# Routing inside cross-attention, four shared-expert groups ahead of the blocks, silu transposes a block later, four result pairs

## The reference

```
x = x + attn(layernorm(x))        # delta-rule attention and a gated MLP of width 512
x = x + xattn(layernorm(x), ctx, ctx, mask)   # 16 heads of 16, 375 keys per row
x = x + ffn(layernorm(x))

def ffn(x):                       # N_EXPERTS = 6, TOP_K = 2
    probs = sigmoid(xt @ gate_w.T + gate_b)
    w, idx = top_k(probs, 2);  w = w / (sum(w) + 1e-08)
    y = sum over e of ge[:, e] * ((silu(xt @ ew1[e].T) * (xt @ ew3[e].T)) @ ew2[e].T)
    z = (silu(xt @ fc1.T) * (xt @ fc2.T)) @ fc3.T      # the shared expert, for all tokens
    return y + z
```

## Time and profile before

| | |
|---|---|
| runs | median 1516.21 us of three (1514.62 to 1520.04) |
| profiled execution | 1508.45 us, its span 1506.7 us |
| busy over the span | PE 1323.7 us (88%), DVE 914.1 (61%), ACT 651.0 (43%), POOL 420.4 (28%) |
| mean granted TensorE clock | 0.931 |
| chain that ended last | PE 68%, DVE 8%, issue 7%, POOL 7% |

### The profile page before, as it was taken

How to read it: one execution, slowest core, us unless ns; L and a number is a source line. 1 busy time by engine, 2 the same in 40 slices (tenths; PEclk the granted TensorE clock), 3 DMA queues, 4 the chain that set the end, 5 groups by cost and what they waited for, 6 DMA issues and landing times.

```text
span 1506.7 us, 33730 instructions
## 1 busy us (share of the span) xinstructions
PE 1323.7 (88%) x11138; PEld 1181.8 (78%) x11138; DVE 914.1 (61%) x2823; ACT 651.0 (43%) x1474; POOL 420.4 (28%) x387
## 2 busy tenths in 40 slices
PE   5899999999898699999999999999974538898997
PEld 5888998898887588888888888888764427777886
DVE  5677567557545366666666666666656624544577
ACT  3534334434332255555555555555531214444532
POOL 2323224223312311111111111111116642332353
PEclk9999999999898699999999999999975559999999
DMA  7799100000002545455555555554114322322255
GB/s 181 156 225 231 48 0 0 0 0 0 20 11 49 144 120 117 118 119 119 119 120 118 119 119 119 119 119 118 45 32 131 109 68 75 93 79 84 80 129 168
DMA packets 117837, 143.96 MB, mean 96 GB/s; under 512 B 24112, under 2 KB 101280, under 8 KB 117744
## 3 DMA queue, kind: packets, MB, share of 16 engines
q1 hardware_dynamic: 111024, 127.21, 36.2%
q0 software_dynamic: 6160, 15.69, 3.1%
q10 hardware_dynamic: 576, 0.07, 0.0%
HBM read 75.61 MB, written 42.15 MB: 78 GB/s over the span
## 4 chain that ended last, share of the span: by engine, by line
PE 68%; DVE 8%; issue 7%; POOL 7%; SPq 3%; DMA 2%; ACT 2%; POOLq 0%; DVEq 0%; ACTq 0%
PE psum L725 19%; PE psum L961 7%; PE psum L1124 6%; PE psum L995 5%; PE psum L976 5%; PE psum L981 5%; POOL routed_h L671 4%; PE psum L1143 3%; SPq L465 2%; PE psum L846 2%; PE psum L832 2%; PE psum L933 2%; PE psum L843 2%; PE psum L1133 2%; PE psum L1022 1%
## 5 line engine op out<-in xcount | busy, mean ns | idle before, releaser
L1824 DVE CUSTOM_DVE_ANT_0 junk<-psum,biasq 112x375 f32<-112x375 f32 x512 | 270.2, 547 | 114.6 <-PE psum L961 77.5
L1432 ACT ACTIVATE pr<-psum 125x448 f32<-125x448 f32 x384 | 202.4, 544 | 115.1 <-PE psum L981 106.6
L981 PE MATMUL psum<-qst,kst 97*125 97x224 f32 x768 | 226.0, 353 | 0.0
L961 PE MATMUL psum<-kst,qst 96*112 96x376 f32 x512 | 185.9, 371 | 12.4 <-DVE smax L1824 10.8
L981 PEld LDWEIGHTS psum<-qst,kst 97*125 97x125 f32 x768 | 146.4, 191 | 7.9
L976 PE MATMUL psum<-flagk,negbig 125*125 125x448 bf16 x384 | 139.2, 363 | 3.5 <-DMA qst<-negm 3.3
L566 POOL TENSOR_TENSOR rs<-rs,neg_half 112x1 f32<-112x1 f32 x32 | 18.2, 569 | 386.8 <-DVE rs L1802 386.8
L961 PEld LDWEIGHTS psum<-kst,qst 96*112 96x112 f32 x512 | 91.3, 178 | 42.1 <-DVE smax L1824 37.2
L686 POOL DMA_INDIRECT routed_y<-yb,yrow x61 | 59.1, 969 | 146.9 <-DVE yrow L2086 117.9
L995 PE MATMUL psum<-pr,vaug 125*32 125x112 f32 x3072 | 93.7, 262 | 0.0
L995 PEld LDWEIGHTS psum<-pr,vaug 125*32 125x32 f32 x3072 | 70.3, 110 | 15.3 <-issue 6.3
(11 more groups left out here) (308 smaller groups left out, 3381.8 us busy)
## 6 DMA issues: line engine op xcount, KB each, us to landing
kst<-khi SPq DMA_DIRECT2D x64, 376.0 KB, 5.2
routed_h<-in_route_pad SPq DMA_DIRECT2D x6, 3640.0 KB, 43.2
kst<-klo SPq DMA_DIRECT2D x32, 376.0 KB, 6.8
ctxT<-in_ctxT SPq DMA_DIRECT2D x32, 375.0 KB, 5.2
hblk<-routed_h SPq DMA_DIRECT2D x61, 130.0 KB, 2.1
qst<-qhi SPq DMA_DIRECT2D x128, 56.0 KB, 2.1
h<-routed_y SPq DMA_DIRECT2D x16, 448.0 KB, 5.1
stage<-in_e SPq DMA_DIRECT2D x21, 256.0 KB, 3.3
```

The lines of the kernel that those rows point to most:

```text
L961: pe.matmul(bank[max_bank(n, hd)][0:T, 0:S2E], head(qst[par][0:ROWS], hd), pair(kst[par][0:ROWS], hd // 2), start=True, stop=True).then_in ...
L981: mm = pe.matmul(bank[q % 3][0:KP, cols(i, 2 * T)], pair(kst[par], n)[:, cols(q // HPB, KP)], both(qst[par], n), start=False, stop=True, s ...
L1432: nc.scalar.activation(pr[q % PROBS][:].rearrange("k i q -> k (i q)"), bank[q % 3][0:KP, 0:GT], ACT.Exp, scale=1.0 / HD ** 0.5).then_inc(s ...
L1824: nc.vector.tensor_tensor_reduce(out=junk[:, hd % 2, :], in0=bank[max_bank(n, hd)][0:T, 0:S2], in1=biasq[:, par, :], scale=1.0, scalar=-3e ...
```

## The change

**Routing row by row.** `transpose_row`, `route` and `place` on PE, `moments3`, `normalise3`, `add_gate_bias`, `sigmoid` (now with the engine's search for the eight largest and their positions in place of comparisons and ranks) and `slots` on DVE, `exponential_gate` and `keep_h` on ACT, and `decide` and `scatter` on POOL stand inside the step of cross-attention, for the row one to three behind. DVE's own `normalise` is cut in two: `moments` at q == 5, `scale_row` at the end. The transposed rows no longer stay on chip: SP writes each to DRAM (`store_turned`) and reads them back by groups for the shared expert (`load_turned`).

**Shared groups ahead.** Groups 0 to 3 (`FRONT` = 4) of the shared expert run after the last row, between the last rows' routing and the splitting of the experts' weights; groups 4 to 7 stay behind the blocks.

**Blocks.** `transpose_hidden` and `contract_block` run one block later than before against `expand_block`, with the other engines' parts.

**Results.** The pairs of result rows have a ring of four (over the experts' weights, free by then) in place of two.

```diff
+FRONT = 4
...
+            def store_turned(t, par):
+                r = t * RB + par
+                sp.wait_ge(s3["sent"], 16 * (r + 1))
+                sp.wait_ge(s3["hall"], r + 1)
+                sp.dma_start(turned[bass.ds(r, 1)].rearrange("a c p t -> p (a c) t"), hT3[par][:]).then_inc(s3["sent"], 16)
+
+            def load_turned(g):
+                sp.wait_ge(s3["sent"], 16 * (GB * (g + 1) + 1))
...
+                for c in range(DC):
+                    sp.dma_start(to[:, c], turned[group(g), c].rearrange("j p t -> p j t")).then_inc(s3["ht_in"], 16)
...
             def load_products(g):
-                if g >= 2:
-                    sp.wait_ge(s3["x_new"], 2 * (g - 2) + 1)
+                if g >= RINGS:
+                    sp.wait_ge(s3["x_new"], added("routed", g - RINGS))
...
+            load_turned(6)
             for n in range(RINGS):
                 sp.wait_ge(s4[f"out{n}"], ring_turn(NBLK - 1 - (NBLK - 1 - n) % RINGS))
-            load_products(0)
-            load_products(1)
+            for g in range(RINGS):
+                load_products(g)
+            load_turned(7)
             for g in range(G):
-                if g + 2 < G:
-                    load_products(g + 2)
-                sp.wait_ge(s3["x_new"], 2 * (g + 1))
+                if g + RINGS < G:
+                    load_products(g + RINGS)
+                sp.wait_ge(s3["x_new"], max(added("routed", g), added("shared", g)))
...
+            def decide(t, par):
...
+                count_choice(b)
+                nc.gpsimd.tensor_scalar(told(par, C_TOKEN), told(par, C_TOKEN), float(RB * T), None, ALU.add).then_inc(s3["gating"], 1)
+                wait_apart(pool, s3["prob"], SORTING * (b + 1))
+                nc.gpsimd.tensor_copy(told(par, C_EXPERT), pick[:, 0:1]).then_inc(s3["gating"], 1)
+                nc.gpsimd.tensor_copy(second[:], pick[:, 1:2]).then_inc(s3["gating"], 1)
...
+                nc.gpsimd.tensor_scalar(hot[:, 0], line[0:T, R_EXPERT:R_EXPERT + NE], told(par, C_EXPERT), None, ALU.is_equal).then_inc(s3["gating"], 1)
...
+                nc.gpsimd.tensor_scalar(hot[:, 1], line[0:T, R_EXPERT:R_EXPERT + NE], second[:, 0:1], None, ALU.is_equal).then_inc(s3["gating"], 1)
...
+                nc.gpsimd.tensor_tensor(chosen[:], hot[:, 0], hot[:, 1], op=ALU.add).then_inc(s3["gating"], 1)
+                nc.gpsimd.tensor_tensor(top[:, 2:3], top[:, 0:1], top[:, 1:2], op=ALU.subtract).then_inc(s3["gating"], 1)
...
+                nc.gpsimd.tensor_scalar(told(par, C_SECOND, 2), top[:, 1:3], total[:, 0:1], None, ALU.mult).then_inc(s3["gating"], 1)
...
+            def landed(t, par):
+                wait_apart(pool, s3["scat"], 16 * TOP * (t * RB + par + 1))
+
+            def scatter(t, par):
+                c = t * RB + par
+                pool.wait_ge(s3["slot"], 3 * (c + 1))
+                wait_apart(pool, s3["gating"], DECIDED * (c + 1))
+                for r in range(TOP):
+                    to = bass.IndirectOffsetOnAxis(ap=slot[par][:, r:r + 1], axis=0)
+                    pool.indirect_dma_start(hbuf[:, :], to, h3[par][:], None).then_inc(s3["scat"], 16)
...
+            def step(t, par, masks=True, power=True):
+                early = t * RB + par if isinstance(t, int) else RB
+                if masks:
+                    mask_bias(*ahead(t, par, 2))
+                if early >= 3:
+                    scatter(*ahead(t, par, -3))
                 if power:
                     rsqrt(*ahead(t, par, 3))
+                if early >= 2:
+                    decide(*ahead(t, par, -2))
+                if early >= 1:
+                    rsqrt3(*ahead(t, par, -1))
+                if early >= 3:
+                    landed(*ahead(t, par, -3))
...
+            def transpose_row(t, par):
+                r = t * RB + par
+                pe.wait_ge(s["h1"], G + r + 1)
...
+                for c in range(DC):
+                    mm = pe.transpose(bank[DENSE[0]][:, cols(c)], h3[par][:, cols(c, P)], ident[0:T, 0:T])
+                mm.then_inc(s["ht_ps"], 1)
+
+            def route(t, par):
+                b = t * RB + par
+                pe.wait_ge(s3["hall"], b + 1)
...
+                for c in range(DC):
+                    mm = pe.matmul(bank[small_banks(b)[0]][0:T, 0:NE], hT3[par][:, c], router[:, c], start=c == 0, stop=c == DC - 1)
+                mm.then_inc(s3["lg_ps"], 1)
+
+            def place(t, par):
+
+                b = t * RB + par
+                pe.wait_ge(s3["gating"], DECIDED * b + 7)
...
+                pe.matmul(to, earlier[0:T, 0:T], chosen[:], start=True, stop=False)
+                pe.matmul(to, earlier[:, T:2 * T], counted[:], start=False, stop=True).then_inc(s3["place_ps"], 1)
...
+                    if q == 0 and early >= 2:
+                        route(*ahead(t, par, -2))
+                    if q == 9 and early >= 2:
+                        place(*ahead(t, par, -2))
+                    if q == 10 and early >= 1:
+                        transpose_row(*prev)
...
                 for i in range(NBLK):
                     expand_block(i, owners[i])
                     if i > 0:
-                        contract_block(i - 1, owners[i - 1])
+                        transpose_hidden(i - 1)
                     if i + 2 < NBLK:
                         transpose_block(i + 2)
-                    transpose_hidden(i)
+                    if i > 1:
+                        contract_block(i - 2, owners[i - 2])
...
+            half_shared(0, 0, 0)
             transpose_o(ROUNDS + 1, 1)
-            route(0)
+            half_shared(0, 0, 1)
             transpose_on(ROUNDS + 1, 1)
+            route(*ahead(ROUNDS + 1, 1, -1))
+            half_shared(0, 1, 0)
             project_out(ROUNDS + 1, 1)
-
-            for g in range(G):
-                if g + 1 < G:
-                    transpose_group(g + 1)
-                    route(g + 1)
-                places(g)
+            half_shared(0, 1, 1)
+            half_shared(1, 0, 0)
+            half_shared(1, 0, 1)
+            transpose_row(ROUNDS + 1, 1)
+            half_shared(1, 1, 0)
+            half_shared(1, 1, 1)
+            place(*ahead(ROUNDS + 1, 1, -1))
+            contract_shared(0)
+            route(ROUNDS + 1, 1)
+            expand_shared(2)
+            contract_shared(1)
+            half_shared(3, 0, 0)
+            half_shared(3, 0, 1)
+            place(ROUNDS + 1, 1)
+            half_shared(3, 1, 0)
+            half_shared(3, 1, 1)
+            contract_shared(2)
             totals()
+            contract_shared(3)
             routed_blocks()
...
+            def keep_h(t, par):
+                r = t * RB + par
+                act.wait_ge(s["ht_ps"], G + r + 1)
...
+                nc.scalar.copy(hT3[par][:], bank[DENSE[0]][:, 0:2 * T]).then_inc(s3["hall"], 1)
+
+            def exponential_gate(t, par):
+                act.wait_ge(s3["prob"], SORTING * (t * RB + par) + 1)
+                nc.scalar.activation(prob[:, 0:NE], logit[:], ACT.Exp, scale=-1.0).then_inc(s3["ex"], 1)
...
+                    if q == 2 and early >= 2:
+                        exponential_gate(*ahead(t, par, -2))
...
+                    if following == 0 and 3 <= q < 3 + NE:
+                        high_expert(q)
+                    if q == 11 and early >= 1:
+                        keep_h(*prev)
...
                 if i > 0:
-                    scale_block(i - 1)
-                high_hidden_block(i)
+                    high_hidden_block(i - 1)
                 if i + 2 < NBLK:
                     high_block(i + 2)
-            high_shared(1)
+                if i > 1:
+                    scale_block(i - 2)
+            high_hidden_block(NBLK - 1)
+            scale_block(NBLK - 2)
             scale_block(NBLK - 1)
...
+            def moments3(t, par):
...
+            def normalise3(t, par):
+                r = t * RB + par
+                dve.wait_ge(s["rs1"], G + r + 1)
+                nc.vector.tensor_scalar(h3[par][:, 0:D], x_row(r), mv[:, 1, 0:1], rs[:, 1, 0:1], ALU.subtract, ALU.mult).then_inc(s["h1"], 1)
+
+            def add_gate_bias(t, par):
+                b = t * RB + par
+                dve.wait_ge(s3["lg_ps"], b + 1)
+                nc.vector.tensor_tensor(logit[:], bank[small_banks(b)[0]][0:T, 0:NE], gateb[:], op=ALU.add).then_inc(s3["prob"], 1)
+
+            def sigmoid(t, par):
+                b = t * RB + par
+                dve.wait_ge(s3["ex"], b + 1)
+                nc.vector.tensor_scalar(prob[:, 0:NE], prob[:, 0:NE], 1.0, None, ALU.add).then_inc(s3["prob"], 1)
...
+                nc.vector.reciprocal(prob[:, 0:NE], prob[:, 0:NE]).then_inc(s3["prob"], 1)
+                wait_apart(dve, s3["prob"], SORTING * b + 3)
+                if not isinstance(b, int) or b > 0:
+                    wait_apart(dve, s3["gating"], DECIDED * b)
+                nc.vector.max(top[:], prob[:]).then_inc(s3["prob"], 1)
+                wait_apart(dve, s3["prob"], SORTING * b + 4)
```

(67 more changed lines are left out.)

685 lines of the change are left out of this document (348 added, 337 removed).

## The result

The changed kernel takes 1579.2 us (median of four runs, 1577.0 to 2132.7; in one run the clock was far lower, and it is left out of the comparison, as is one run of e3 of 2440.7 us) against 1515.4 us: ratio 1.0415, 95% interval 1.0379 to 1.0451. It is slower by 63 us; forecast were 59 us less. The profiled execution took 1581.15 us, its span 1578.8.

What follows compares the result with a forecast made beforehand. PE was taken to bound cross-attention, while POOL's serial scatters held up routing. Terms 49 - 74 - 10 - 24 = -59 us, from 1516.2, gave 1457 us; range 1418 to 1497.

Steps and rivals of the forecast that it cites:

- What bounds the kernel, and its views: Stage-by-stage reading: PE sets cross-attention's pace; in routing, POOL's 64 scatters run one behind another for 80 us.
- Term 1: Cross-attention steps: routing work moved into each row costs 1.65 us a row, +49 us in all, bounds +17 to +76.
- The burst reaching PE at head 10: Cross-attention: six `sigmoid` operations on DVE ahead of head 8 delay PE by 1.5 us less 0.4, +1.1 a row.
- the rival in which POOL shuts DVE out: Cross-attention: POOL delays DVE's `clo`, and head 0 with it, in every row: +36 us, 1493 us; chance 0.14.
- Term 2: From the last row to the first block: 129.3 us shrink to 55.5, -74 us, bounds -83 to -62.
- the 5 us for crowding: Between last row and first block: 5 us added because low parts on POOL and DVE crowd each other.
- the prediction's rule on the port: VectorE and GpSimd share a port pair: a VectorE operation with two SBUF inputs waits out a GpSimd operation reading SBUF.
- Term 3: Blocks: the silu transposes' wait for DVE's product goes, 0.21 us for each of 60; -10 us, bounds 0 and -14.
- The 3 us taken back for the tighter ring: Blocks: the ring of four `hblk` loads gets tighter by 1.3 us, so 3 us of gain were given up.
- Term 4: Tail: PE loses four groups, transfers then set a length of about 51 us; -24 us, bounds -30 and 0.
- `decide` was never late: Rival in cross-attention: `decide` on POOL comes late and PE's `place` waits, +77 us, 1534 us; chance 0.07.
- The slower side: Whole kernel: the chance that the changed kernel measures slower than before, put at 0.07.

Runs made afterwards that it cites:

- e3: Changed kernel with DVE's cross-attention loop written out and `sigmoid` moved from slot 3 to slot 6: 1500.37 us, ratio 0.9904 to the kernel before.
- e13: Changed kernel unaltered, run again on another chip: 1550.25 us, ratio 1.0244 to the kernel before.
- e5: Changed kernel with six products that nobody reads on PE ahead of head 10, to fill the pause: 1553.45 us, ratio 1.0238.
- e2: Changed kernel with DVE's `sigmoid` in slot 6 instead of slot 3: 1538.07 us, ratio 1.0148.
- e6: Kernel before, its DVE loop lengthened by 30 instructions a row that only test a semaphore long passed: 1556.40 us, ratio 1.0264.
- e1: Changed kernel with DVE's loop over the middle rounds of cross-attention written out: 1523.95 us, ratio 1.0071.
- e12: Changed kernel with the silu transposes and a block's contraction back where they stood before: 1565.19 us, ratio 1.0331.
- e14: Changed kernel with a ring of two result pairs instead of four, on the same chip as e13: 1553.90 us, ratio 1.0256.
- e7: As e3, but with `sigmoid` in slot 7 behind `add_row`: 1495.78 us, ratio 0.9868.
- e10: As e7, plus POOL's scatters at its step's end, POOL's loop written out, DVE's tail reordered, `transpose_row` in slot 11: 1467.54 us, ratio 0.9688.

## Why the prediction was wrong

**What bounds the kernel, and its views** were read rightly: PE sets cross-attention's pace.

**Term 1 failed**: +49 forecast, +17 to +76 its bounds. In `after` it was +171 (4.6 + 156.0 + 10.4), on e13's chip about +140. Its parts:
- *The burst reaching PE at head 10*: place and size right (1.39 and 1.71 us; 1.5 less 0.4 forecast). PE's own products cost 0.12 (`place`) + 0.19 (`transpose_row`) + 0.41 (`route`) = 0.7 us, not 0.55.
- *Missing: the half clock.* I priced waits as if PE went on at full speed behind them. e5 and e13 give 1.3 us a middle row; e2 took pause and echo away together.
- *Missing: the jump back.* I wrote that DVE has room in sum and asked what each added instruction takes, never how many there are. e6: 41 us with no work added, some 32 of them at the ends of rounds, more than all of PE's products.
- *Missing: the late heads 3 to 5*, 27 us (754.4 - 727.2), on some chips. Nearest was the rival in which POOL shuts DVE out, at `clo` and with +36; the delay came at other instructions. In `after`, `clo` itself never waited for POOL: it takes 0.94 us in every row, and ACT ended each wait ahead of it.
- These don't simply add: e1 and e2 alone gained 57 and 41 us of rows, together 77, probably since each removal also spares half clock elsewhere.

**Term 2 held** in its total: -71 (-74 forecast), 60 us from the last values product to the first expansion (55.5). Its parts did less well, and the 5 us for crowding made up for some of it. The recorded items add up to 35.5 us, not 36.4; the plan starts at 43.2 us and takes 7.6, not 4.3. One operation of it is why, 0.33 us before and 3.82 after:

```profile
1208.62 0.33 DVE L2020 TENSOR_TENSOR blocks<-count,line 128x168 f32<-128x168 f32 x1
```

```profile
1317.78 3.82 DVE L2214 TENSOR_TENSOR blocks<-count,line 128x168 f32<-128x168 f32 x1
```

POOL runs two low parts of 2.1 us each there, back to back until 1321.40, and `blocks` ends 0.2 us behind them. This is the prediction's rule on the port, on the chain to the first block, in 3.5 us.

**Term 3 held**: -15 (-10). e12 puts 15.9 us on the block order. The 3 us taken back for the tighter ring were not needed.

**Term 4 was mis-sized**: -13 (-24). The estimate had the transfers never idle from the first moment. POOL's first addition starts when the first pair has landed, at 1529.79, 19 us behind the start of the last expansion. That four pairs are issued together is not why: with two (e14) it is 18.1 us, with four on the same chip (e13) 18.5. DVE stands for that addition with the silu product of the next group queued behind, as DVE's and PE's rows of `after` show:

```profile
1532.16 3.08 DVE L2193 TENSOR_TENSOR x_res<-x_res,e_hi 112x1024 f32<-112x1024 f32 x1 [10.34 <-POOL e_hi L828]
```

```profile
1541.49 1.08 PE L1305 MATMUL psum<-h3hi,sh_hi 128*128 128x448 f32 x2 [14.18 <-DVE hid L2169]
```

Four of the eight additions on DVE took 3.1 to 3.4 us, 1.22 undisturbed. Each of the four ends 1.1 us behind an operation of POOL, the mark of the prediction's rule on the port.

**The rivals.** `decide` was never late in the rows (no wait at `place` up to the last row in any trace; behind it e7 to e10 have two of 1.6 to 1.9 us each). The slower side came, but by mechanisms that no rival named, so 0.07 for slower was too sure: the chance was built over known mechanisms alone.

## What to carry to other kernels

When work is put into a loop of an engine, count the loop's instructions as well as their time, and look in the profile whether the instruction queue moves in the middle of the loop; if it does, write the loop out or shorten it. Where PE runs gapless, price a pause like the 1.39 us here at its length and 1.3 to 1.7 us more for the half clock that may follow; waits of 0.47 to 0.95 us a row (e3, the middle rows of e6) kept the clock. Put bursts of small operations where the engine has nothing late behind it: moving four groups of instructions and writing two loops out gave back more than the 63 us lost. The step from 1.0415 to 0.9688 holds the chips' difference, too: on e10's chip the changed kernel with a ring of two stands at 1.0252.

## What was not expected of the hardware

- A DVE loop of 341 or 343 instructions fetches five blocks of 8192 bytes in each turn and stands 2.2 to 3.2 us at its end; one of 253 fetches none.
- The same pause is not always followed by half clock. In e1, with 1.25 us in each, rows of 21.8 us at full clock and of 23.1 at 0.93 stand side by side. In e13 PE stands 1.39 us at 770.83 and this window behind it is at full clock, where `after` fell to 0.50:

```profile
771.00:776.90 5.90, 5.79 (x62) 4.74 (x62) 5.01 (x21) 2.33 (x5) 1.87 (x7) 1.00 0.48 100
```

  In `after` heads 3 to 5 had been late just ahead of the pause. So, as it seems, the 27 us of the late heads are part waiting (0.6 us a row) and part half clock: over 440 us (640 to 1080) the clock is 0.89 in `after` and 0.92 in e13.
- One program differed by 1.9% between two sets of runs (1.7% in the ratio to the kernel before), through a delay of 0.85 us at three instructions of a row, while the kernel before didn't differ.
